# Graph attention on one core: two element-by-element passes of VectorE issued in pieces of 256 elements instead of 1024

## The reference, cut to what matters

```python
h = jnp.einsum('nf,fhd->nhd', x, W)                 # 8 heads of 32
a_src = jnp.sum(h * att_src, axis=-1)
a_dst = jnp.sum(h * att_dst, axis=-1)
e = jax.nn.leaky_relu(a_src[src] + a_dst[dst], NEG_SLOPE)
e_max = jax.ops.segment_max(e, dst, num_segments=N)
e_exp = jnp.exp(e - e_max[dst])
...
msg = h[src] * alpha[:, :, None]
out = jax.ops.segment_sum(msg, dst, num_segments=N)
```

## Time and profile before

| what | before |
|---|---|
| time, median of 3 runs | 3578.34 us (3570.36 to 3581.91) |
| the profiled execution | 3579.75 us |
| its span, first to last instruction | 3578.0 us |
| POOL busy | 1991.3 us, 56% |
| DVE busy | 1708.5 us, 48% |
| PE busy | 2507.4 us, 70% |

### The profile page before, as it was taken

One profiled execution on the slowest core, in us unless ns is written; L12 is line 12 of the kernel. 1 busy time (PEld: TensorE's weight loads), 2 busy tenths in 40 slices (PEclk: granted clock), 3 DMA queues, 4 the chain that ended last, 5 costly groups with the idle time before them and its releaser, 6 DMA issues. The chain is left out here.

```text
span 3578.0 us, 49607 instructions
## 1 busy us (share of the span) xinstructions
PE 2507.4 (70%) x12468; PEld 1999.4 (56%) x12469; DVE 1708.5 (48%) x3583; ACT 974.1 (27%) x1944; POOL 1991.3 (56%) x2005
## 2 busy tenths in 40 slices
PE   5466555566655552999924888888888878639993
PEld 4344444444444352888824776777677754427772
DVE  5466666676666682111166444444444444621115
ACT  4300000000000031544443233333333324624441
POOL 0577777777777356222204777777777730463331
PEclk9687888787887755999967999999999989769996
DMA  5444444444444235222255555555555510242226
GB/s 154 123 129 130 127 128 129 129 133 132 128 127 128 70 110 204 81 78 83 77 188 164 155 156 158 157 157 158 158 157 152 157 54 2 94 162 83 88 89 245
DMA packets 319883, 459.13 MB, mean 128 GB/s; under 512 B 56729, under 2 KB 213962, under 8 KB 319498
## 3 DMA queue, kind: packets, MB, share of 16 engines
q0 software_dynamic: 94560, 261.75, 24.5%
q1 hardware_dynamic: 212888, 180.18, 16.9%
q10 hardware_dynamic: 12276, 15.62, 1.3%
HBM read 376.96 MB, written 80.39 MB: 128 GB/s over the span
## 5 line engine op out<-in xcount | busy, mean ns | idle before, releaser
L604 POOL DMA_INDIRECT room<-h_table,src_idx x784 | 837.7, 1068 | 354.4 <-issue 238.5
L2153 POOL DMA_INDIRECT em_msg<-xn_table,src_idx x784 | 746.8, 953 | 337.2 <-issue 238.5
L1105 PE MATMUL at_ps<-room,at_member 128*128 128x264 f32 x1584 | 495.3, 466 | 91.4 <-DVE room L961 88.7
L2229 PE MATMUL em_pse<-em_We,em_attr_t 128*128 128x256 f32 x1552 | 397.4, 414 | 158.3 <-DVE em_msg L2177 158.3
L2177 DVE TENSOR_TENSOR em_msg<-em_pse,em_msg 128x1024 f32<-128x1024 f32 x196 | 230.8, 1219 | 548.2 <-DMA em_msg<-xn_table,src_idx 548.2
L2229 PEld LDWEIGHTS em_pse<-em_We,em_attr_t 128*128 128x128 f32 x1552 | 312.5, 206 | 227.3 <-DVE em_msg L2177 169.0
L1105 PEld LDWEIGHTS at_ps<-room,at_member 128*128 128x128 f32 x1584 | 341.8, 227 | 173.6 <-DVE room L961 100.5
L2282 ACT ACTIVATE em_msg<-em_msg 128x1024 f32<-128x1024 f32 x196 | 207.2, 1057 | 682.5 <-DVE em_msg L2177 675.3
L2236 PE MATMUL em_psa<-em_msg,em_member 128*128 128x256 f32 x1584 | 359.7, 380 | 2.1 <-DVE acc L2187 2.1
L2236 PEld LDWEIGHTS em_psa<-em_msg,em_member 128*128 128x128 f32 x1584 | 302.1, 191 | 43.8 <-DVE acc L2187 2.5
L1785 POOL DMA_INDIRECT y_table<-room,m0e_dest x104 | 99.7, 958 | 298.3 <-DVE room L1805 292.9
(11 more groups left out here) (395 smaller groups left out, 3928.6 us busy)
## 6 DMA issues: line engine op xcount, KB each, us to landing
em_attr<-in_edge_attr_dram SPq DMA_DIRECT2D x97, 512.0 KB, 4.2
room<-x_sorted SPq DMA_DIRECT2D x105, 258.0 KB, 2.7
at_dst_row<-dst_flat SPq DMA_DIRECT2D x98, 256.0 KB, 3.8
room<-h_table,src_idx POOLq DMA_INDIRECT x784
at_resets<-reset_flat SPq DMA_DIRECT2D x784, 8.0 KB
em_msg<-xn_table,src_idx POOLq DMA_INDIRECT x784, 2.8
room<-in_x_dram SPq DMA_DIRECT2D x12, 896.0 KB, 10.3
cn_rows<-y_table SPq DMA_DIRECT2D x5, 1792.0 KB, 10.2
```

What stands on the lines that cost most here:

```text
L604: pool.indirect_dma_start(msg[:, s, j, :], None, mem.h_table[:, :], bass.IndirectOffsetOnAxis(ap=mem.src_idx[:, c:c + 1].bitcast(u32), axi ...
L1105: ins = nc.tensor.matmul(ps_a[:, which, 0:MSG], member[which][:, j, :], msg[:, s, c, :], start=(j == 0), stop=(j == CB - 1))
L2153: pool.indirect_dma_start(msg[:, s, j, :], None, mem.xn_table[:, :], bass.IndirectOffsetOnAxis(ap=mem.src_idx[:, c:c + 1].bitcast(u32), ax ...
L2229: ins = nc.tensor.matmul(ps_e[h][:, j, :], attr_t[:, s % 2, c * P:(c + 1) * P], We[:, :], start=True, stop=True)
```

## The change

`mark` issues four instructions of two chunks (256 elements for each partition) in place of one of eight chunks. `weigh` issues four instructions of one chunk (256 elements) in place of one of four chunks. The semaphore is raised by the last piece alone, so nothing that waits for a mark or a weighing is told earlier. The elements, their order and the engine stay the same, and no other instruction is moved. In a step DVE issues 8 marks in place of 2, and 16 weighings in place of 4.

```diff
             def mark(dst, b, r):
-                return nc.vector.scalar_tensor_tensor(dst[:, :, :], mem.iota_row[:, :].unsqueeze(1).to_broadcast([P, CB, P]),
-                                                      col(mem.neg_base, r),
-                                                      cols(mem.key_e, b * CB, CB).unsqueeze(2).to_broadcast([P, CB, P]),
-                                                      op0=ALU.subtract, op1=ALU.is_equal)
+                for j in range(0, CB, 2):
+                    ins = nc.vector.scalar_tensor_tensor(dst[:, j:j + 2, :], mem.iota_row[:, :].unsqueeze(1).to_broadcast([P, 2, P]),
+                                                         col(mem.neg_base, r),
+                                                         cols(mem.key_e, b * CB + j, 2).unsqueeze(2).to_broadcast([P, 2, P]),
+                                                         op0=ALU.subtract, op1=ALU.is_equal)
+                return ins
...
             def weigh(k, s, quarter):
                 dve.wait_ge(weighted, k + 1)
-                part = msg[:, s, quarter * HC:(quarter + 1) * HC, :].rearrange("p c (h w) -> p (c h) w", w=HW)
-                nc.vector.tensor_tensor(part[:, :, 0:HD], part[:, :, 0:HD],
-                                        part[:, :, HD:HW].to_broadcast([P, HC * HEADS, HD]), ALU.mult).then_inc(msg_done, 1)
+                for c in range(quarter * HC, (quarter + 1) * HC):
+                    part = msg[:, s, c, :].rearrange("p (h w) -> p h w", w=HW)
+                    ins = nc.vector.tensor_tensor(part[:, :, 0:HD], part[:, :, 0:HD],
+                                                  part[:, :, HD:HW].to_broadcast([P, HEADS, HD]), ALU.mult)
+                ins.then_inc(msg_done, 1)
```

## The result

The changed kernel takes 3587.97 us, median of 20 runs, against 3579.27 us of the kernel before, also 20 runs: ratio 1.0027, 95% interval 1.002 to 1.0034. I had forecast 3517 us. It is slower by 9 us where 62 were to be gained.

What follows compares the result with a forecast made beforehand. POOL's gathers were taken to bound the attention stage. 3579.75 us profiled, minus 64 of gather stretch, plus 2 of DVE work, gave 3517.75, set at 3517 for the median of the runs; range 3488 to 3560 us.

Steps and rivals of the forecast that it cites:

- What bounds, and what stretches a gather: Attention: POOL's gathers set the length; DVE instructions with two SBUF operands hold gathers, about 96 us of stretch.
- Is a piece boundary enough?: Between DVE pieces following at once, a held gather gets in; each piece holds a gather for itself alone.
- My upper bound, 88 us of stretch: Attention gathers: every gather issued inside a train of pieces held a whole 0.27 us window, leaving only 5 us gained.
- the lock outlasts the train: Rival, chance 0.08: a held gather loses every boundary until the last piece ends; +57 us, 3639 us.
- Its sign, a maximum above 2 us: Profile after: a longest gather above 2 us would mean the lock outlasts the pieces; about 1.25 us was forecast.
- What POOL gains: Attention gathers: holds fall to 0.6 us a step, 29 us in all; stretch 96 to 32 us, 64 us gained.
- The formula's premise of random distances: Hold per gather, (L - 0.17)²/2 over gather distance, takes random distances; gave 2.5 us a step where the trace has 1.9.
- What DVE pays: Cut marks and weighings add 1.8 us a step; DVE's chain grows about 1.1 us, from 17.2 to 18.3 us.
- The cover: DVE's longer chain stays hidden by 2.3 us a step of waiting for rows; cost only 2 us at the end.
- POOL's hoped-for 20.6: POOL's attention step after the change: 16 gathers of 0.946 + 0.304 us, 20.0 us, plus 0.6 of holds.

Runs made afterwards that it cites:

- the wait: Changed kernel plus a DVE wait for its own mark's end before each of a step's first two weighings: ratio 0.9909 to the kernel before.
- the memset: Changed kernel plus an unused 400-element memset after each mark, not waited for: ratio 0.9917 to the kernel before.
- The shifted kernel: Kernel before, nothing cut, plus an unused 400-element memset behind each mark: ratio 1.0127.
- half as many ways back: Changed kernel with DVE waiting for the mark's end before the first two weighings, every engine's loop over eight steps instead of four: ratio 0.9855.
- the kernel of one kind: Changed kernel with weighing pieces issued as scalar_tensor_tensor with a pointer to ones, the marks' kind of instruction: ratio 0.9999 to the kernel before.
- eight steps a loop: Changed kernel with every engine's loop over eight steps instead of four and nothing else: ratio 1.003 to the kernel before.

## Why the prediction was wrong, by its own steps

*What bounds, and what stretches a gather.* Right: POOL set the length, and without the second SBUF operand the stretch went from 96 to 9 us and the time to 0.9766.

*"Is a piece boundary enough?"* This step failed. I took one boundary, from a whole mark to a whole weighing, for all boundaries. Those between mark pieces were open in every run, those of the third and fourth weighing too. In the first two weighings, directly behind the marks, 82 gathers were held past their piece, 66.8 us, and six from the last mark piece, 9.7 us; six were let through. My upper bound, 88 us of stretch, took each piece to hold for itself alone and so was passed as well, at 104. This is the rival "the lock outlasts the train", in half of its places: I gave it 0.08 and had it hold everywhere, hence its 3639 us. Its sign, a maximum above 2 us, came: 2.58 us.

*What POOL gains.* With the boundaries opened, by the wait or by the memset, the stretch was 33 and 43 us against the 32 forecast, so the size was about right. How far that is luck is not shown, since in these runs too the gathers fell into the same few places step after step. The formula's premise of random distances hid how much the distances decide. In the kernel before, the first two weighings happened to hold almost no gathers, 6 us. The longer marks moved them onto gathers, just where the boundaries are closed. The shifted kernel shows the size of such moves without any cut, +39 us.

*What DVE pays.* The pieces and the chain were right: 17.2 us to 18.4 (605.60 to 623.97), 18.3 forecast. The cover was not. I read 4.9 us a step of waiting for rows as spare, and overlooked that 1.5 us of it, and about 5.7 at each loop's end, is DVE's own time for registers and branches, hidden as long as rows are late. DVE's own least step was about 20.8 us in the changed kernel (18.3 + 2.5), not 18.3, and so already above POOL's hoped-for 20.6. That is a second failed step. It cost nothing in the changed kernel, whose gathers came slower still. It shows once they are free: 0.9909, and 0.9855 with half as many ways back.

With both failures mended the change gives 0.9855, 52 us, where 62 were forecast. The wait's 0.2 us twice a step is in that.

*Left open.* Why a boundary closes. Shown: all boundaries that passed a gather over lie at or behind a mark, in the first two trains, save those from a train to the `mark_t` behind it in the kernel of one kind. The train behind a step's second mark was closed whether that mark was cut or whole; the one behind the first mark was closed when the mark was cut, but for a few gathers in its second and third piece, and let gathers through when it was whole. Mark pieces do not close among themselves, and a whole weighing behind a whole mark let gathers through. A wait, with a memset or without, opens the boundary from mark to train, and with the memset it opens the train inside. Within one and the same piece, gathers issued up to 0.23 us before its end were let through and those at 0.25 us and more were passed over (with eight steps a loop up to 0.22, and 0.23 and more). So neither the kind of instruction, nor the full queue, nor the mark ahead is the whole reason, and the moment of the issue counts. No run varies that moment alone.

## What to carry to other kernels

If indirect gathers set the pace, look at how far above its median the mean gather is, and lay the slow ones against VectorE's instructions, those with two SBUF operands first. Then take away the second SBUF operand, by putting one in PSUM, and don't cut: the cut costs VectorE time, shifts everything against the gathers, and is good only where boundaries are open. And before an engine's wait is called spare, look at what its queue does in that wait: branches, register loads and the loop's way back need it too.

## What the runs showed of the hardware

- A gather is held by a VectorE instruction with two SBUF tensors and ends 0.82 us after it is let through; the same instruction with one operand in PSUM does not hold it (0.95 us inside a 1.21 us weighing).
- A tensor_scalar with one SBUF tensor held it too (1.20 us in place of 0.95, let through at the end of a `mark_t`, int16 to bf16, 1024 elements in 0.48 us).
- The hold of an instruction can begin before its recorded start: gathers issued 0.35 to 0.37 us before a weighing's were held to its end, those at 0.39 us and more were not.
- A held gather could be passed over at four boundaries in a row (2.56 us, against 0.95 unheld). With a memset of 0.39 us ahead of the train none was.
- The Trainium skill says that a DVE instruction with two SBUF inputs contends with a GpSimd instruction that reads SBUF, and that the shared pair is an exclusive lock (SBUF — State Buffer, "Who interferes with whom"). The runs agree for one instruction. They go beyond it: across a train of four, 82 gathers were held to the end of the train.
- The loop's way back cost VectorE about 4 us each time (idle 5.67 and 5.98 us against 1.5), nearly all of it between the branch and the next row of its queue.
